# The second mixture of a two-layer decoder on one core: each tile's results scattered by POOL to token and choice rows, and loaded back in token order

## The chip, the cores and the metric

The kernel runs on one core of one Trainium2 chip. The time is device microseconds of one execution, and the median of the runs counts. Engines are named as in the profile: PE is TensorE's matmul, PEld its weight load, DVE VectorE, ACT ScalarE, POOL GpSimd, SP SyncE; SPq is SP's DMA queue.

## The reference, cut to what matters

The decoder has two layers over 1024 tokens (4 x 256) of 256 channels. All the work around this change is in its last sublayer, a mixture of 16 experts of which each token takes two, and a shared expert:

```python
logits = flat @ router_w.T
scores = jax.nn.softmax(logits, axis=-1)
_, topk_idx = jax.lax.top_k(logits + router_bias, TOPK)          # TOPK = 2
topk_scores = jnp.take_along_axis(scores, topk_idx, axis=-1)
topk_scores = topk_scores / topk_scores.sum(-1, keepdims=True)
combine = jnp.einsum('nk,nke->ne', topk_scores, jax.nn.one_hot(topk_idx, N_EXPERTS))
for e in range(N_EXPERTS):
    h = jax.nn.silu(flat @ Wu[e]) * (flat @ Wg[e])
    out = out + combine[:, e:e + 1] * (h @ Wd[e])
out = out + jax.nn.silu(flat @ Su[0]) * (flat @ Sg[0]) @ Sd[0]
x = x + out
```

## The kernel before

The program is written out by hand, one instruction stream to an engine, with semaphores between them. `PsumBanks` hands out PSUM's eight banks in the order in which PE claims them; `filled` counts PE's finished banks, in that one order, and `emptied` counts the banks read by ACT and by DVE.

The 2048 (token, choice) pairs of the second mixture are sorted by expert into 31 tiles of 128 slots (`TILES1`); each expert's slots begin at a tile, so slots are left over. DVE works out every pair's slot (`e_slot`, `e_idx`, L1922 to L1938). Two one-hot matrices, `e_A` and `e_B` (L1942 to L1947), let one PE product (`tile_tokens`, L1085) give for every slot its token, which DVE turns into `e_ids` (L1954 to L1956); the expert of each tile goes to `e_eid` (L1948 to L1951). A slot without a pair has token 0.

Then these streams run over the tiles:

- POOL (L2175 to L2185) issues one indirect DMA for each tile, which fetches its 128 token rows of 1 KB from HBM (`xs1`) into one of eight buffers `e_x`. From the ninth on it waits until PE has turned the rows that were in the buffer.
- PE (L1139 to L1147) turns tile j+1's rows, multiplies tile j by its expert's two up weights, turns the hidden rows of tile j-1, and multiplies those of tile j-2 by the down weights (`ex`, `eu`, `eh`, `ey`).
- DVE (L1975 to L1979) copies the turned rows out (`rows_out`) and multiplies gate by up (`gated_tile`). ACT (L1459 to L1465) takes the gate's Silu (`gate`), copies the turned hidden rows (`hidden_out`) and the results (`result_out`), these into one of four buffers `e_y`, for which it waits until the result four tiles back has been sent.
- SP (L2304 to L2306) stores each result, in order of slots, to `ys1` in HBM.

When all 31 results are stored, POOL issues 16 indirect DMAs, two for each of the eight token tiles, that fetch every token's two rows from `ys1` by `e_idx` into `e_yg`. DVE adds each pair with its weights to X (L1991, L1993) and SP stores that token tile.

The shared expert's down product is `shared_down(t)`: t = 0 to 3 ahead of the tile loop, t = 4 to 7 after it; DVE adds each to X (`residual`).

Of the kernel before, what the change touches and what calls it, by code (L numbers as in the profile page):

```python
# [13 lines left out]
P = 128  # L14
F32 = mybir.dt.float32
# [71 lines left out]
def decoder(nc, x, ctx_512, L0_attn_Wk, L0_attn_Wv, L0_attn_Wr, L0_attn_Wo, L0_attn_time_decay, L0_attn_time_first,  # L87
# [5 lines left out]
    with ExitStack() as ctx:  # L93
# [5 lines left out]
        def sem(name):  # L99
            return ctx.enter_context(nc.semaphore(name))  # L100
# [12 lines left out]
        def at(name, offset, shape, dt=F32):  # L113
            size = int(np.prod(shape[1:])) * 4
            assert offset + size <= room, (name, offset + size, room)
            return nc.alloc_sbuf_tensor_at(name, shape, dt, offset=arena + offset)
# [190 lines left out]
        e_hT = at("e_hT", 131072, [P, 2, P])  # L307
        e_y = at("e_y", 132096, [P, 4, C])
        e_yg = at("e_yg", 136192, [P, NT, 2, C])
        xs1 = nc.dram_tensor("token_rows_6", [B * T, C], F32, kind="Internal").ap()  # L310
        ys1 = nc.dram_tensor("tile_results_6", [TILES1 * P, C], F32, kind="Internal").ap()


        filled = sem("bank_filled")
# [33 lines left out]
        res_sent = [sem(f"slot_results_sent_{i}") for i in range(3)]  # L348
        res_back = [sem(f"token_results_loaded_{t}") for t in range(NT)]
        router_loaded = sem("router_loaded")  # L350
        xs1_stored = sem("token_rows_stored")
        choice_ready = sem("two_choices_ready")
        onehot_ready = sem("slot_one_hots_ready")
        eid_ready = sem("tile_experts_ready")
# [152 lines left out]
        def _(pe):  # L507
# [611 lines left out]
            def shared_down(t):  # L1119
                out_product(("sd", t), [(e_hs[:, it, t * P:(t + 1) * P], m_wd[:, E1 + it, :]) for it in range(2)])  # L1120
# [11 lines left out]
            pe.wait_ge(*banks.emptied(("sg", 1)))  # L1132
            for t in range(4):
                shared_down(t)
            pe.wait_ge(eid_ready, 1)
            of_tile = nc.values_load_multi_w_load_instructions(
                e_eid[0:1, 0:TILES1], engines=[mybir.EngineType.PE], min_val=0, max_val=E1 - 1,
                skip_runtime_bounds_check_because="a count of ends among the first 15 experts")[1]
            for j in range(-1, TILES1 + 2):  # L1139
# [5 lines left out]
                    hidden_turned(j - 1)  # L1145
                if 0 <= j - 2:
                    tile_down(j - 2)  # L1147
            pe.wait_ge(*banks.emptied(("sg", 3)))
            for t in range(4, NT):
                shared_down(t)  # L1150
            ended(pe, 5)


# [318 lines left out]
        def _(dve):  # L1472
            steps = [0]

            def link(ins):

                steps[0] += 1
                ins.then_inc(dve_step, 1)
                dve.wait_ge(dve_step, steps[0])
# [42 lines left out]
            def residual(key, t):  # L1522
                ps = banks.take(key, "dve")
                dve.wait_ge(*banks.filled(key))
                V.tensor_tensor(X[:, t, :], X[:, t, :], ps[:, 0:C], ALU.add).then_inc(emptied["dve"], 1)  # L1525
# [191 lines left out]
            def bcast(a, n):  # L1717
                return a.unsqueeze(2).to_broadcast([P, a.shape[1], n])
# [216 lines left out]
                                 e_rank[:, :, :].rearrange("p e t -> p t e").unsqueeze(1).to_broadcast([P, 2, NT, E1]), ALU.mult))  # L1935
            link(V.tensor_reduce(e_slot[:, :, :], e_sel[:, :, :, :], AX, ALU.add))
            slot = e_slot[:, :, :].rearrange("p k t -> p (k t)")
            link(V.tensor_copy(e_idx[:, :], slot))  # L1938
            link(V.tensor_scalar(e_qu[:, :], e_idx[:, :], P - 1, None, ALU.bitwise_and))
            link(V.tensor_copy(e_q[:, :], e_qu[:, :]))  # L1940
            link(V.tensor_tensor(e_jq[:, :], slot, e_q[:, :], ALU.subtract))
            link(V.tensor_tensor(e_one[:, :, :], bcast(e_jq[:, :], 32), e_tiles.unsqueeze(1).to_broadcast([P, 2 * NT, 32]), ALU.is_equal))  # L1942
            V.tensor_scalar(e_A[:, :, 0, :], e_one[:, :, :], e_p, None, ALU.mult)
            V.tensor_tensor(e_A[:, :, 1, :], e_one[:, :, :], bcast(e_high, 32), ALU.mult)
            for k in range(2):
                V.tensor_tensor(e_B[:, NT * k:NT * (k + 1), :], bcast(e_q[:, NT * k:NT * (k + 1)], P),
                                e_iota.unsqueeze(1).to_broadcast([P, NT, P]), ALU.is_equal).then_inc(onehot_ready, 1)  # L1947
            link(V.tensor_tensor(e_past[:, :, :], e_end[:, 0:E1 - 1].unsqueeze(1).to_broadcast([P, 32, E1 - 1]),  # L1948
                                 bcast(e_j, E1 - 1), ALU.is_le))
            link(V.tensor_reduce(e_ef[:, :], e_past[:, :, :], AX, ALU.add))  # L1950
            V.tensor_copy(e_eid[:, :], e_ef[:, :]).then_inc(eid_ready, 1)  # L1951
            ps = banks.take("ids", "dve")
            dve.wait_ge(*banks.filled("ids"))
            V.tensor_reduce(e_idf[:, :], ps[:, 0:64].rearrange("p (s j) -> p j s", s=2), AX, ALU.add).then_inc(emptied["dve"], 1)  # L1954
            dve.wait_ge(*banks.emptied("ids"))
            V.tensor_copy(e_ids[:, :], e_idf[:, :]).then_inc(ids_ready, 1)  # L1956
            for n in range(1, 4):
                hidden(n)
            for t in range(4):
                residual(("sd", t), t)  # L1960
            def rows_out(j):

                if j >= 2:
                    dve.wait_ge(*banks.filled(("eu", j - 2)))
                copy_out(("ex", j), e_xT[:, j % 2, :, :], lambda ps: ps[:, 0:2 * P].rearrange("p (k s) -> p k s", k=KC))
# [9 lines left out]
            for j in range(-1, TILES1):  # L1975
                if j + 1 < TILES1:
                    rows_out(j + 1)
                if j >= 0:
                    gated_tile(j)  # L1979
            for t in range(4, NT):  # L1980
                residual(("sd", t), t)
            dve.wait_ge(e_exp, 2)
            link(V.tensor_tensor(e_sel[:, :, :, :], e_oh[:, :, :, :], f_e[:, :, :].unsqueeze(1).to_broadcast([P, 2, NT, E1]), ALU.mult))
            link(V.tensor_reduce(e_s[:, :, :], e_sel[:, :, :, :], AX, ALU.add))
# [2 lines left out]
            link(V.tensor_tensor(e_w[:, :, :], e_s[:, :, :], e_sum[:, :].unsqueeze(1).to_broadcast([P, 2, NT]), ALU.mult))  # L1987
            for t in range(NT):
                dve.wait_ge(*banks.emptied(("sd", t)))
                dve.wait_ge(both_back[t], 32)  # L1990
                V.scalar_tensor_tensor(X[:, t, :], e_yg[:, t, 0, :], e_w[:, 0, t:t + 1], X[:, t, :], ALU.mult, ALU.add).then_inc(both_added, 1)  # L1991
                dve.wait_ge(both_added, t + 1)
                V.scalar_tensor_tensor(X[:, t, :], e_yg[:, t, 1, :], e_w[:, 1, t:t + 1], X[:, t, :], ALU.mult, ALU.add).then_inc(x_final, 1)  # L1993
# [4 lines left out]
        def _(pool):  # L1998
# [173 lines left out]
            link(G.memset(y_wop[:, :, :, :], 0.0))  # L2172
            for ot in range(KC):
                G.tensor_copy(y_wop[:, ot, :, 0:16], y_wo[:, ot, :].rearrange("p (h d) -> p h d", h=H)).then_inc(wo_padded, 1)
            pool.wait_ge(xs1_stored, 32)  # L2175
            pool.wait_ge(ids_ready, 1)
            for j in range(TILES1):
                if j >= 8:
                    pool.wait_ge(*banks.filled(("ex", j - 8)))
                G.indirect_dma_start(e_x[:, j % 8, :], None, xs1, IndirectOffsetOnAxis(ap=e_ids[:, j:j + 1], axis=0)).then_inc(tile_back[j % 8], 16)  # L2180
            for i in range(4):
                pool.wait_ge(tile_sent[i], 16 * len(range(i, TILES1, 4)))
            for t in range(NT):
                for k in range(2):
                    G.indirect_dma_start(e_yg[:, t, k, :], None, ys1, IndirectOffsetOnAxis(ap=e_idx[:, k * NT + t:k * NT + t + 1], axis=0)).then_inc(both_back[t], 16)  # L2185
            ended(pool, 5)


# [1 line left out]
        def _(sp):  # L2190
# [109 lines left out]
            for g in range(2):  # L2300
                sp.wait_ge(hn_ready, NT * 5 + 4 * (g + 1))
                sp.dma_start(xs1[4 * g * P:4 * (g + 1) * P, :].rearrange("(t p) c -> p t c", p=P),
                             HN[5][:, 4 * g:4 * (g + 1), :]).then_inc(xs1_stored, 16)
            for j in range(TILES1):  # L2304
                sp.wait_ge(*banks.emptied(("ey", j)))
                sp.dma_start(ys1[j * P:(j + 1) * P, :], e_y[:, j % 4, :]).then_inc(tile_sent[j % 4], 16)  # L2306
            for t in range(NT):
                sp.wait_ge(x_final, t + 1)
                sp.dma_start(ov[t], X[:, t, :]).then_inc(stored, 16)
# [3 lines left out]
def shape_constants():  # L2313

    f = np.float32

    def angles(n, dim, base):
        inv = f(1.0) / np.power(f(base), np.arange(0, dim, 2, dtype=f) / f(dim), dtype=f)
        return np.arange(n, dtype=f)[:, None] * inv[None, :]

    c = {"ident_c": np.eye(P, dtype=f)}
    a = np.repeat(angles(T, QW, 10000.0), 2, axis=-1)
    cos, sin = np.cos(a), np.sin(a)

    half = QW // 2
    other = np.concatenate([sin[:, half:], -sin[:, :half]], axis=-1)
    pair = lambda t: np.tile(np.concatenate([t.T[i] for i in (slice(0, P), slice(0, P), slice(P, QW), slice(P, QW))])
                             .reshape(3, P, T).transpose(1, 0, 2), (1, 1, 2))
    c["cosq_c"], c["sinq_c"] = pair(cos), pair(other)
    a = np.zeros((LT * P, D), f)  # L2330
    a[:L] = np.repeat(angles(L, D, 10000.0), 2, axis=-1)
    sign = np.concatenate([-np.ones(D // 2, f), np.ones(D // 2, f)])
    rows = lambda t: t.reshape(LT, P, D).transpose(1, 0, 2)
    c["cosk_c"], c["sink_c"] = rows(np.cos(a)), rows(np.sin(a) * sign)
    rev = np.arange(E1, 0, -1, dtype=f)
    c["rev_c"] = np.broadcast_to(rev, (P, NT, E1))
    row = lambda a: np.broadcast_to(np.asarray(a, f), (P, len(a)))
    tri = np.triu(np.ones((P, P), f), 1)
    c["tri_c"] = np.concatenate([
        tri, row(np.arange(P)), row(P * np.arange(32)), row(np.arange(32)), np.arange(P, dtype=f)[:, None],  # L2340
        row(P * np.tile(np.arange(NT), 2)), row(P * np.arange(8)), row(np.tile(np.arange(NT) > 0, E1)), tri - 1], axis=1)
    a = angles(T, P, 1000000.0)
    rows = lambda t: np.concatenate([t, t], -1).reshape(2, P, P).transpose(1, 0, 2)
    sign = np.concatenate([-np.ones(P // 2, f), np.ones(P // 2, f)])
    c["cos1_c"], c["sin1_c"] = rows(np.cos(a)), rows(np.sin(a)) * sign
    tri = np.where(np.arange(P)[None, :] > np.arange(P)[:, None], f(NEG), f(0.0))
    c["mask_c"] = tri
    c["hmask_c"] = (np.arange(P)[:, None] // 16 % 2 == np.arange(2)[None, :]).astype(f)
    return {k: np.ascontiguousarray(v, dtype=f) for k, v in c.items()}
# [32 lines left out]
```

## Time and profile before

| | |
|---|---|
| median of 3 runs | 1368.84 us (1368.06 to 1370.04) |
| span of the profiled execution | 1379.6 us |
| busy: PE, DVE, ACT, POOL | 1272.7, 868.2, 634.6, 824.0 us |
| first fetch of a tile's rows on POOL | 1285.76 us |
| last result stored | 1354.07 us (1352.38 and 1.69) |
| first and last fetch of results on POOL | 1354.89 and 1373.67 us |

The record gives no other time of the profiled execution than its span. The span is 10.8 us above the median. Times in rows are microseconds from the span's start; "idle before" is given in square brackets with what ended it. A chain is followed back from the last instruction of the program.

### The profile page before, as it was taken

The page shows a single profiled execution, that of the slowest core. Times are in us where ns is not written, and L with a number is a line of the kernel's source. Part 1 is how long each engine was busy: PE and PEld are TensorE (multiplying, and loading weights), DVE is VectorE, ACT ScalarE, POOL GpSimd, SP SyncE. Part 2 cuts the span into 40 slices and gives each one's busy share as a digit, 9 for nine tenths or more (in the row PEclk, how much of TensorE's full clock was granted, in tenths as well). Part 3 has the DMA queues.
Part 4 walks back from the last instruction along what each step waited for, and adds up shares of the span by engine and source line. Part 5 has one row for each costly group of instructions (what it writes and reads, how often), then busy time and mean ns, then how long its engine had stood idle before and what let it go on. Part 6 is the DMA issues. An engine that isn't in the chain of part 4 may idle for free.

```text
span 1379.6 us, 20358 instructions
## 1 busy us (share of the span) xinstructions
PE 1272.7 (92%) x7123; PEld 826.8 (60%) x7123; DVE 868.2 (63%) x1490; ACT 634.6 (46%) x1687; POOL 824.0 (60%) x748
## 2 busy tenths in 40 slices
PE   7999997999999999999999758998999999989792
PEld 4865554666666666666668643445776874556582
DVE  4756666677777777778865636675666123664443
ACT  3731123445554455544551416887665115872151
POOL 1267005799999999999993445887444004560444
PEclk9999997999999999999999888999999997998897
DMA  9501111000000000000005620000000105200263
GB/s 261 134 9 32 37 31 27 9 8 9 9 11 10 9 9 9 10 11 9 9 5 176 195 65 2 1 1 1 1 1 1 27 1 155 63 1 32 69 142 118
DMA packets 66172, 58.91 MB, mean 43 GB/s; under 512 B 19424, under 2 KB 62968, under 8 KB 65560
## 3 DMA queue, kind: packets, MB, share of 16 engines
q1 hardware_dynamic: 62952, 49.09, 12.7%
q0 software_dynamic: 3120, 8.52, 2.6%
q8 instruction: 58, 0.95, 0.3%
q14 instruction: 42, 0.34, 0.1%
HBM read 40.69 MB, written 8.52 MB: 36 GB/s over the span
## 4 chain that ended last, share of the span: by engine, by line
PE 79%; DVE 6%; ACT 5%; POOL 4%; issue 4%; DMA 1%; DVEq 0%; SPq 0%; POOLq 0%; ACTq 0%
PE PS L515 73%; PE PS L523 5%; ACT s_sc L1402 2%; POOL a_m L2137 2%; POOL a_m L2131 2%; DVE s_mx L1859 1%; ACT a_m L1356 1%; DVE pm L1622 1%; DVE HN L1504 0%; PE PS L729 0%; DMA f_xg<-token_rows,f_ids 0%; POOL s_sc L2152 0%; PE PS L685 0%; POOL f_xg L2119 0%; PE PS L623 0%
## 5 line engine op out<-in xcount | busy, mean ns | idle before, releaser
L2080 POOL TENSOR_TENSOR PWS<-PWS 128x1024 f32<-128x1024 f32 x160 | 379.7, 2373 | 45.1 <-ACT PWS L1286 25.8
L1622 DVE TENSOR_REDUCE pm<-PS 128x2 f32<-128x1024 f32 x192 | 225.8, 1218 | 69.3 <-PE PS L515 68.7
L1286 ACT ACTIVATE PWS<-PS 128x512 f32<-128x512 f32 (+1 forms) x416 | 213.3, 599 | 78.4 <-PE PS L515 78.2
L515 PE MATMUL PS<-PWS,KVR 128*64 128x256 f32 (+1 forms) x1664 | 185.8, 380 | 0.0
L515 PE MATMUL PS<-QALL,KH 128*128 128x512 f32 (+1 forms) x416 | 182.6, 439 | 0.9 <-DVE QM L1646 0.9
L515 PE MATMUL PS<-QM,KL 68*128 68x512 f32 (+1 forms) x416 | 167.3, 402 | 0.0
L2152 POOL TENSOR_SCALAR s_sc<-s_sc,s_ri 128x128 f32<-128x128 f32 (+1 forms) x256 | 104.5, 429 | 98.9 <-DVE s_ri L1866 98.9
L515 PEld LDWEIGHTS PS<-PWS,KVR 128*64 128x64 f32 (+1 forms) x1664 | 121.4, 137 | 59.0 <-issue 0.9
L515 PEld LDWEIGHTS PS<-QALL,KH 128*128 128x128 f32 (+1 forms) x416 | 77.9, 187 | 76.9 <-ACT PWS L1286 57.4
L1402 ACT ACTIVATE s_sc<-PS,s_nb 128x128 f32<-128x128 f32 (+1 forms) x256 | 104.5, 433 | 3.9 <-DVE s_nb L1862 3.9
L1859 DVE TENSOR_REDUCE s_mx<-PS 128x2 f32<-128x512 f32 (+2 forms) x112 | 65.7, 611 | 50.1 <-PE PS L515 50.0
L515 PE MATMUL PS<-KH,QALL 64*128 64x512 f32 (+1 forms) x512 | 89.3, 408 | 7.0 <-DVE pm L1622 7.0
L515 PE MATMUL PS<-a_wT,HT 128*128 128x512 f32 x192 | 93.4, 620 | 0.7 <-issue 0.7
L1297 ACT ACTIVATE QALL<-CTX 128x256 fp32r<-128x256 f32 x32 | 13.3, 417 | 154.0 <-DVE CTX L1659 154.0
L515 PEld LDWEIGHTS PS<-QM,KL 68*128 68x128 f32 (+1 forms) x416 | 79.0, 190 | 6.2
L515 PEld LDWEIGHTS PS<-KH,QALL 64*128 64x128 f32 (+1 forms) x512 | 46.9, 189 | 43.7 <-issue 26.0
L515 PE MATMUL PS<-z_HTh,z_w 128*128 128x512 f32 x192 | 67.5, 420 | 2.4 <-DVEq L502 2.4
L2180 POOL DMA_INDIRECT e_x<-token_rows,e_ids x31 | 29.5, 951 | 67.2 <-DVE e_ids L1956 46.8
L2131 POOL TENSOR_TENSOR a_m<-a_m,a_m 128x512 f32<-128x512 f32 x40 | 51.0, 1276 | 29.5 <-DVE a_m L1836 29.5
L1271 ACT ACTIVATE QALL<-PS 64x512 fp32r<-64x512 f32 x32 | 19.0, 594 | 106.3 <-PE PS L515 105.9
L1525 DVE TENSOR_TENSOR X<-X,PS 128x256 f32<-128x256 f32 x40 | 16.8, 419 | 76.8 <-PE PS L515 76.7
L1390 ACT ACTIVATE s_pt<-PS 128x512 f32<-128x512 f32 x64 | 38.5, 602 | 53.6 <-PE PS L523 53.6
(328 smaller groups left out, 2518.3 us busy)
## 6 DMA issues: line engine op xcount, KB each, us to landing
QALL<-qlo SPq DMA_DIRECT2D x32, 128.0 KB, 2.4
QM<-QALL SPq DMA_DIRECT2D x64, 64.0 KB, 2.0
f_w<-in_L_ffn_w_dram SPq DMA_DIRECT2D x2, 2048.0 KB
tile_results<-e_y SPq DMA_DIRECT2D x31, 128.0 KB
a_nat<-in_L_attn_w_qkv_dram SPq DMA_DIRECT2D x1, 3072.0 KB, 13.0
x_wq<-in_L_xattn_Wq_dram SPq DMA_DIRECT2D x1, 2048.0 KB, 10.4
x_wo<-in_L_xattn_Wo_dram SPq DMA_DIRECT2D x2, 1024.0 KB, 6.9
a_wo<-in_L_attn_w_o_dram SPq DMA_DIRECT2D x1, 2048.0 KB, 17.5
```

The lines of the kernel that those rows point to most:

```text
L515: return nc.tensor.matmul(o, a, b, start=start, stop=stop, **kw)
L523: last = nc.tensor.transpose(ps[0:w, c:c + r], a, ident[0:r, 0:r])
L1286: nc.scalar.activation(PW[c][0:rows, j * HALF:(j + 1) * HALF], st_bank("block", LT * u + lt)[0:rows, :], ACT.Exp).then_inc(p_ready, 1)
L1390: nc.scalar.activation(s_pt[:, m % 2, 0, :], ps, ACT.Copy).then_inc(emptied["act_turned"], 1)
L1402: ins = nc.scalar.activation(s_sc[:, k % 4, h, 0:nk], ps[:, j * nk:(j + 1) * nk], ACT.Exp, bias=s_nb[:, k % 3, h:h + 1], scale=scale, accu ...
L1622: V.tensor_reduce(pm[u % 2][:, :, i // 3, i % 3], src, AX, ALU.max).then_inc(nat_read, 1)
L1859: ins = V.tensor_reduce(s_mx[:, k % 3, i * per:(i + 1) * per], banks.bank(key)[:, 0:per * nk].rearrange("p (h k) -> p h k", h=per), AX, AL ...
L2080: G.tensor_tensor(ACC[:, :], PW[0][:, :] if i == 0 else ACC[:, :], PW[i + 1][:, :], ALU.add).then_inc(acc_step, 1)
L2131: G.tensor_tensor(a_m1[:, n % 6, :], a_m1[:, n % 6, :], a_m2[:, n % 2, :], ALU.add).then_inc(m_sum, 1)
L2137: G.tensor_tensor(m1, m1, a_bt[:, i, s, :].unsqueeze(1).to_broadcast([P, 4, P]), ALU.add).then_inc(qk_ready, 1)
L2152: ins = G.tensor_scalar(s_sc[:, n % 4, h, 0:nk], s_sc[:, n % 4, h, 0:nk], s_ri[:, n % 4, h:h + 1], 1.0, ALU.mult, ALU.mult)
L2180: G.indirect_dma_start(e_x[:, j % 8, :], None, xs1, IndirectOffsetOnAxis(ap=e_ids[:, j:j + 1], axis=0)).then_inc(tile_back[j % 8], 16)
```

## The change

- Each result is no longer stored by SP in order of slots. POOL issues one indirect DMA for each tile that writes its 128 rows to row `choice * 1024 + token` of a larger `ys1`. To this end the one-hot product's value is now that row plus one (`scalar_tensor_tensor` for `e_A`, and a constant row that numbers the pairs 0 to 2047). A slot without a pair gives 0 and gets a row of its own behind the 2048 (`e_dump`, `e_miss`). The row to fetch is the lower ten bits (`e_tok`).
- POOL issues the first eight fetches, and then, tile by tile, the fetch of tile j+8 and the scatter of tile j-3.
- After all scatters SP loads the results with eight plain DMAs, 256 KB each, one for each token tile.
- The tile experts `e_eid` are worked out ahead of the one-hot matrices, not after them. All eight `shared_down` and their `residual` run ahead of the tile loop.

```diff
@@ tensor
             for t in range(4):
                 shared_down(t)
+            pe.wait_ge(*banks.emptied(("sg", 3)))
+            for t in range(4, NT):
+                shared_down(t)
             pe.wait_ge(eid_ready, 1)
...
-            pe.wait_ge(*banks.emptied(("sg", 3)))
-            for t in range(4, NT):
-                shared_down(t)
             ended(pe, 5)
@@ vector
-            link(V.tensor_copy(e_idx[:, :], slot))
+            V.tensor_copy(e_idx[:, :], slot).then_inc(idx_ready, 1)
+            dve.wait_ge(idx_ready, 1)
+            link(V.tensor_tensor(e_past[:, :, :], ..., ALU.is_le))
+            link(V.tensor_reduce(e_ef[:, :], e_past[:, :, :], AX, ALU.add))
+            V.tensor_copy(e_eid[:, :], e_ef[:, :]).then_inc(eid_ready, 1)
...
-            V.tensor_scalar(e_A[:, :, 0, :], e_one[:, :, :], e_p, None, ALU.mult)
+            V.scalar_tensor_tensor(e_A[:, :, 0, :], e_one[:, :, :], e_p, e_one[:, :, :], ALU.mult, ALU.add)
...
-            link(V.tensor_tensor(e_past[:, :, :], ..., ALU.is_le))
-            link(V.tensor_reduce(e_ef[:, :], e_past[:, :, :], AX, ALU.add))
-            V.tensor_copy(e_eid[:, :], e_ef[:, :]).then_inc(eid_ready, 1)
+            V.tensor_scalar(e_dump[:, :], e_tiles, e_p, float(2 * B * T + 1), ALU.add, ALU.add)
             ps = banks.take("ids", "dve")
...
-            V.tensor_copy(e_ids[:, :], e_idf[:, :]).then_inc(ids_ready, 1)
+            link(V.scalar_tensor_tensor(e_miss[:, :], e_idf[:, :], 0.0, e_dump[:, :], ALU.is_equal, ALU.mult))
+            link(V.scalar_tensor_tensor(e_idf[:, :], e_idf[:, :], -1.0, e_miss[:, :], ALU.add, ALU.add))
+            link(V.tensor_copy(e_ids[:, :], e_idf[:, :]))
+            V.tensor_scalar(e_tok[:, :], e_ids[:, :], B * T - 1, None, ALU.bitwise_and).then_inc(ids_ready, 1)
             for n in range(1, 4):
                 hidden(n)
-            for t in range(4):
+            for t in range(NT):
                 residual(("sd", t), t)
...
-            for t in range(4, NT):
-                residual(("sd", t), t)
...
-                dve.wait_ge(both_back[t], 32)
+                dve.wait_ge(both_back[t], 16)
@@ gpsimd
+            def rows_fetched(j):
+                if j >= 8:
+                    pool.wait_ge(*banks.filled(("ex", j - 8)))
+                G.indirect_dma_start(e_x[:, j % 8, :], None, xs1, IndirectOffsetOnAxis(ap=e_tok[:, j:j + 1], axis=0)).then_inc(tile_back[j % 8], 16)
+            def result_sent(j):
+                pool.wait_ge(*banks.emptied(("ey", j)))
+                G.indirect_dma_start(ys1, IndirectOffsetOnAxis(ap=e_ids[:, j:j + 1], axis=0),
+                                     e_y[:, j % 4, :], None).then_inc(tile_sent[j % 4], 16)
             pool.wait_ge(xs1_stored, 32)
             pool.wait_ge(ids_ready, 1)
-            for j in range(TILES1):
-                if j >= 8:
-                    pool.wait_ge(*banks.filled(("ex", j - 8)))
-                G.indirect_dma_start(e_x[:, j % 8, :], None, xs1, IndirectOffsetOnAxis(ap=e_ids[:, j:j + 1], axis=0)).then_inc(tile_back[j % 8], 16)
-            for i in range(4):
-                pool.wait_ge(tile_sent[i], 16 * len(range(i, TILES1, 4)))
-            for t in range(NT):
-                for k in range(2):
-                    G.indirect_dma_start(e_yg[:, t, k, :], None, ys1, IndirectOffsetOnAxis(ap=e_idx[:, k * NT + t:k * NT + t + 1], axis=0)).then_inc(both_back[t], 16)
+            for j in range(8):
+                rows_fetched(j)
+            for j in range(TILES1 + 3):
+                if j + 8 < TILES1:
+                    rows_fetched(j + 8)
+                if j >= 3:
+                    result_sent(j - 3)
@@ sync
-            for j in range(TILES1):
-                sp.wait_ge(*banks.emptied(("ey", j)))
-                sp.dma_start(ys1[j * P:(j + 1) * P, :], e_y[:, j % 4, :]).then_inc(tile_sent[j % 4], 16)
+            for i in range(4):
+                sp.wait_ge(tile_sent[i], 16 * len(range(i, TILES1, 4)))
+            for t in range(NT):
+                both = ys1[0:2 * B * T, :].rearrange("(k t p) c -> t p k c", k=2, p=P)
+                sp.dma_start(e_yg[:, t, :, :], both[t]).then_inc(both_back[t], 16)
```

## Rows read from the trace of the kernel before

**Rows 1.** The page's first line.

```profile
span 1379.6 us, 20358 instructions
```

**Rows 2.** The chain that ended last: start, length, what.

```profile
1352.38 1.69 DMA tile_results<-e_y
...
1358.64 2.76 DMA e_yg<-tile_results,e_idx
```

**Rows 3.** PE's timeline, turning of rows: start, length, line, operation, count, idle before.

```profile
1311.19 0.38 PE L523 MATMUL PS<-ident,e_x 128*128 128x128 f32 x2
...
1346.99 0.38 PE L523 MATMUL PS<-ident,e_x 128*128 128x128 f32 x2
```

**Rows 4.** POOL's timeline: fetches of rows (L2180) and of results (L2185).

```profile
1285.76 1.06 POOL L2180 DMA_INDIRECT e_x<-token_rows,e_ids  x1 [46.81 <-DVE e_ids L1956]
...
1299.64 0.95 POOL L2180 DMA_INDIRECT e_x<-token_rows,e_ids  x1 [0.30 <-issue]
1303.12 0.95 POOL L2180 DMA_INDIRECT e_x<-token_rows,e_ids  x1 [2.53 <-PE PS L523]
...
1354.89 0.95 POOL L2185 DMA_INDIRECT e_yg<-tile_results,e_idx  x1 [19.32 <-DMA tile_results<-e_y]
...
1373.67 0.95 POOL L2185 DMA_INDIRECT e_yg<-tile_results,e_idx  x1 [0.30 <-issue]
```

**Rows 5.** The timeline of all engines, fifth tile: PE's turning, DVE's copy.

```profile
1294.58 0.38 PE L523 MATMUL PS<-ident,e_x 128*128 128x128 f32 x2
...
1302.95 0.42 DVE L1486 COPY e_xT<-PS 128x256 f32<-128x256 f32 x1 [4.46 <-PE PS L523]
```

**Rows 6.** DVE's timeline from the one-hot matrices to the slots' tokens.

```profile
1279.94 0.35 DVE L1943 TENSOR_SCALAR e_A<-e_one,e_c 128x512 bf16<-128x512 bf16 x1
1280.20 0.68 DVE L1944 TENSOR_TENSOR e_A<-e_one,e_c 128x512 bf16<-128x512 bf16 x1
...
1283.08 0.65 DVE L1948 TENSOR_TENSOR e_past<-e_end,e_c 128x480 f32<-128x480 f32 x1
...
1284.54 0.22 DVE L1954 TENSOR_REDUCE e_idf<-PS 128x32 f32<-128x64 f32 x1
1284.80 0.18 DVE L1956 CAST e_ids<-e_idf 128x32 uint32<-128x32 f32 x1
```

**Rows 7.** PE's timeline ahead of the tile loop.

```profile
1283.58 0.63 PE L515 MATMUL PS<-e_A,e_B 128*128 128x64 bf16 x16
1285.62 3.72 PE L515 MATMUL PS<-m_wd,e_hs 128*128 128x256 f32 x16 [1.41 <-DVE e_hs L1902]
1289.28 0.44 PE L523 MATMUL PS<-ident,e_x 128*128 128x128 f32 x2
```

**Rows 8.** The tile view of `f_xg`, the first mixture's fetches: min/median/max ns.

```profile
L2119 POOL DMA_INDIRECT f_xg<-token_rows,f_ids x10: 945/1058/2129, 772.0 to 786.9; - x10
```

**Rows 9.** DMA issues of the whole run: count, KB each, median us to landing.

```profile
m_wd<-in_L_ffn_Wd_dram SPq DMA_DIRECT2D x1, 2048.0 KB, 8.7
```

**Rows 10.** DVE's timeline, the adds of the results.

```profile
1359.00 0.48 DVE L1991 SCALAR_TENSOR_TENSOR X<-e_yg,e_w,X 128x256 f32<-128x256 f32 x1 [1.78 <-DMA e_yg<-tile_results,e_idx]
1359.52 0.48 DVE L1993 SCALAR_TENSOR_TENSOR X<-e_yg,e_w,X 128x256 f32<-128x256 f32 x1
...
1376.96 0.48 DVE L1993 SCALAR_TENSOR_TENSOR X<-e_yg,e_w,X 128x256 f32<-128x256 f32 x1
```

**Rows 11.** DMA queue of POOL, 1280 to 1380 us: packets, MB, share of 16 engines.

```profile
q0 software_dynamic: 2256, 6.16, 27.7%
```

**Rows 12.** Windows: us, busy and count of PE, PEld, DVE, ACT, POOL, PE's clock, DMA.

```profile
1290.00:1300.00 10.00, 6.16 (x29) 4.35 (x29) 2.23 (x7) 1.11 (x4) 7.56 (x9) 0.96 0.38 106
1300.00:1310.00 10.00, 8.12 (x24) 6.01 (x25) 2.05 (x6) 3.00 (x11) 3.42 (x4) 0.53 0.38 106
```

**Rows 13.** PE's timeline, turning of rows, seventh and eighth tile.

```profile
1306.45 0.64 PE L523 MATMUL PS<-ident,e_x 128*128 128x128 f32 x2
...
1309.56 0.38 PE L523 MATMUL PS<-ident,e_x 128*128 128x128 f32 x2
```

More of the change, by code:

```diff
@@ L309, in decoder @@
         e_yg = at("e_yg", 136192, [P, NT, 2, C])
+        e_dump = at("e_dump", 144384, [P, 32])
+        e_tok = at("e_tok", 144640, [P, 32], U32)
+        e_miss = at("e_miss", 144512, [P, 32])
         xs1 = nc.dram_tensor("token_rows_6", [B * T, C], F32, kind="Internal").ap()
-        ys1 = nc.dram_tensor("tile_results_6", [TILES1 * P, C], F32, kind="Internal").ap()
+        ys1 = nc.dram_tensor("choice_results_6", [(2 * NT + TILES1) * P, C], F32, kind="Internal").ap()
         filled = sem("bank_filled")
@@ L350, in decoder @@
         router_loaded = sem("router_loaded")
-        xs1_stored = sem("token_rows_stored")
+        xs1_stored = sem("slot_rows_stored")
+        idx_ready = sem("choice_slots_ready")
         choice_ready = sem("two_choices_ready")
@@ L1937, in _ @@
             slot = e_slot[:, :, :].rearrange("p k t -> p (k t)")
-            link(V.tensor_copy(e_idx[:, :], slot))
+            V.tensor_copy(e_idx[:, :], slot).then_inc(idx_ready, 1)
+            dve.wait_ge(idx_ready, 1)
+            link(V.tensor_tensor(e_past[:, :, :], e_end[:, 0:E1 - 1].unsqueeze(1).to_broadcast([P, 32, E1 - 1]),
+                                 bcast(e_j, E1 - 1), ALU.is_le))
+            link(V.tensor_reduce(e_ef[:, :], e_past[:, :, :], AX, ALU.add))
+            V.tensor_copy(e_eid[:, :], e_ef[:, :]).then_inc(eid_ready, 1)
             link(V.tensor_scalar(e_qu[:, :], e_idx[:, :], P - 1, None, ALU.bitwise_and))
@@ L1947, in _ @@
                                 e_iota.unsqueeze(1).to_broadcast([P, NT, P]), ALU.is_equal).then_inc(onehot_ready, 1)
-            link(V.tensor_tensor(e_past[:, :, :], e_end[:, 0:E1 - 1].unsqueeze(1).to_broadcast([P, 32, E1 - 1]),
-                                 bcast(e_j, E1 - 1), ALU.is_le))
-            link(V.tensor_reduce(e_ef[:, :], e_past[:, :, :], AX, ALU.add))
-            V.tensor_copy(e_eid[:, :], e_ef[:, :]).then_inc(eid_ready, 1)
+            V.tensor_scalar(e_dump[:, :], e_tiles, e_p, float(2 * B * T + 1), ALU.add, ALU.add)
             ps = banks.take("ids", "dve")
@@ L2340, in shape_constants @@
         tri, row(np.arange(P)), row(P * np.arange(32)), row(np.arange(32)), np.arange(P, dtype=f)[:, None],
-        row(P * np.tile(np.arange(NT), 2)), row(P * np.arange(8)), row(np.tile(np.arange(NT) > 0, E1)), tri - 1], axis=1)
+        row(P * np.arange(2 * NT)), row(P * np.arange(8)), row(np.tile(np.arange(NT) > 0, E1)), tri - 1], axis=1)
     a = angles(T, P, 1000000.0)
```

## The prediction

> **What bounds the kernel now.** The span [rows 1] says what the sum is made against, and the chain that ended last [rows 2] shows where to look: behind the last result's store (1352.38 + 1.69 = 1354.07) it runs through POOL's fetches of results to the end. So I read the timelines of the last hundred microseconds, engine by engine. The reader is to see two regimes. In the tile loop PE sets the pace: 22 tiles from 1311.19 to 1346.99 are 1.627 us each [rows 3]. POOL needs less for its one fetch per tile and waits for PE. After the loop POOL sets the pace: from the first to the sixteenth fetch of results 18.78 us pass, 1.252 us each [rows 4], and DVE and SP follow at that pace.
>
> One stretch needs care. PE turned the fifth tile's rows at 1294.58, but the two that wait for this, DVE's copy [rows 5] and POOL's thirteenth fetch [rows 4], began at 1302.95 and 1303.12. Some 8 us went by, and no row names a cause. Without it the last tile, 26 tiles later, would have been turned at 1294.58 + 26 x 1.627 = 1336.9 and not at 1346.99 [rows 3]: 10.1 us. The span is 10.8 us above the median of the runs. I take this as a sign that timed executions lack the stretch: 1379.6 - 10.1 = 1369.5, 0.7 us above the median of 1368.84. Below, 1369.5 stands for the kernel before, and what I work out for the changed one is lowered by 0.7.
>
> **What comes ahead of the tiles.** The three tile-expert operations now run before the one-hot matrices: 1283.08 to 1284.54 is 1.46 us [rows 6]. `e_A`'s first half becomes a three-operand instruction; bounds are its present 0.35 and the 0.68 of its neighbour of the same size [rows 6], and I take the neighbour, +0.33. The one-hots so end 1.79 later, at 1284.9. The tile experts had hidden PE's wait for them: the product ended at 1283.58 + 0.63 = 1284.21 [rows 7], the reduction began at 1284.54. With half of the 16 products (0.32) behind the later one-hots it begins at 1285.4, 0.9 later. Three more linked steps follow, each like reduction to cast, 0.26 [rows 6]: 0.78. `e_dump` is hidden behind the product. POOL's first fetch moves from 1285.76 [rows 4] by 1.7 to 1287.4 (bounds: +0.8, if only the steps count; +2.6, if nothing is hidden).
>
> PE's eight `shared_down` start 1.7 later, too, and the four that are moved ahead double 3.72 [rows 7]: 1285.62 + 1.7 + 7.44 = 1294.7 for the first turning, against 1289.28. At the end they cost nothing before: POOL's fetches hid them. Now they hide behind POOL as well, if the next step holds.
>
> **POOL in the loop.** It loses 16 fetches and gains 31 scatters. The trace has no scatter. Its nearest rows are fetches with the same 128 rows of 1 KB and the same column of indices: 0.95 us, 1.252 from one to the next [rows 4]. The first mixture's ten took 0.945 to 2.129, median 1.058 [rows 8]; nothing excludes less than 0.945. I take 1.252. A tile then costs POOL 2.504 us, more than PE's 1.627, and POOL becomes the bound. It issues twelve fetches before its first scatter, until 1287.4 + 12 x 1.252 = 1302.4. The first result needs four steps of PE behind 1294.7, 6.5 us: 1301.2. So POOL doesn't wait there, and issues 62 DMAs without a break: the last begins at 1287.4 + 61 x 1.252 = 1363.8. What is queued behind POOL: `result_out` on ACT waits until the scatter four tiles back has landed, and ACT's gates stand behind it, so PE keeps at most three tiles ahead. After the last fetch (51st issue, 1350.0) eleven scatters come at 1.252; eight results are due in that time, 13.0 us at PE's pace against 13.8, so POOL still doesn't wait. PE, ACT and DVE are hidden behind POOL throughout; SP's 31 stores, removed, were hidden but for the last.
>
> On the transfers: POOL's 47 DMAs took 27.7% of 16 engines in 100 us, 0.59 us each [rows 11], half of what their issue takes. The Trainium skill, page "DMA: Bandwidth & Descriptors", section "Issuing engines are not separate DMA queues", says that all DMAs run on the same 16 engines, and that the sequencer's time to start one, which other issuing engines would save, is usually small beside the DMA itself. By it the move of 31 stores to POOL would cost next to nothing, and the sum would be the faster rival's below; the rows say that here the issue is the larger part.
>
> **The end.** The last scatter lands like a fetch, 2.76 after its start [rows 2]: 1366.6 (a store landed in 1.69, a lower bound). SP then loads. The first 256 KB I take at the same 2.76: 1369.3. All 2 MB may take the 8.7 of another 2 MB load [rows 9], until 1375.3. DVE's two adds for a token tile start 0.52 apart [rows 10], 1.03 a tile, 8.24 in all, until 1377.6; that is later than the last load and its pair, so DVE sets this stretch. From the last add's end, 1376.96 + 0.48, to the span's end were 2.16 us [rows 10, 1]. Sum: 1379.7, 10.2 above 1369.5. In the removed part 16 fetches of 1.252, 20.0 us, are gone; POOL's 46 extra issues in and beyond the loop give back more.
>
> **Rivals.** *Faster: issue does not bound.* If a fetch and a scatter together take POOL no more than 1.627, PE bounds the loop. The last result, 1354.07 - 10.1 - 1.69 = 1342.3 before, comes 5.4 later (1294.7 for 1289.28): 1347.7. With 0.3 to start, 2.76 to land, and 13.2 for loads, adds and store (2.76 + 8.24 + 2.16) the end is 1364.0, the time 1363.3. For: the transfer's 0.59. Against: sixteen and thirty-one issues that all took 0.95. Break-even lies at a last scatter begun at 1353.6, which is 1.085 an issue. This is what that page's rule would give.
>
> *The unexplained stretch is real.* If timed runs have it before and after, the first result comes at 1309.2, POOL waits 6.8, and the span is 1386.5 against 1379.6: +6.9, 1375.7. If only the changed kernel has it: 1385.8. If only the old one has it, 1379.7 meets 1379.6: no change, 1368.9. For: ten issues in a row came before it, and POOL now issues in a row throughout. Against: the median.
>
> *PE's clock.* With 1.627 of work in 2.504 PE is 65% busy. Ahead of 1300 it was busy 6.16 of 10 us, and the granted clock was 0.53 in the next ten [rows 12], nearly all at the lower of its two levels (1.2 of 2.4 GHz). There two tiles were 3.11 apart [rows 13], more than 2.504. Ten such microseconds in the steady part cost 10 x (1 - 2.504/3.11) = 1.9 of PE's lead of up to 7.5, so nothing. Behind 1350.0, where PE must follow at 1.627, they cost 10 x (1 - 1.627/3.11) = 4.8: 1383.8. Low for all tiles: 1294.7 + 31 x 3.11 + 9.3 for the pipeline's three steps + 2.76 + 13.2 = 1416.
>
> *A dearer scatter.* At the first mixture's median of 1.058 [rows 8], 31 x 0.11 = 3.4 more: 1382.4; at its longest, 37 more.
>
> **How the numbers follow.** The forecast is POOL's chain without a break, 1379.7 - 0.7 = 1379.0; chance 0.58, own range 1374 to 1384 (an issue 5% cheaper or dearer is 3.9 us, the head's bounds +-0.9). The stretch in the changed kernel, with or without the old: 0.10. The clock: 0.13. A dearer scatter: 0.07. The stretch in the old alone: 0.05. Issue that does not bound: 0.07. A difference under 0.2%, 2.7 us, is about what a measurement of this kernel can't tell from none. Faster has the last case, 0.07. Same has the stretch in the old alone and an issue near break-even, 0.05 + 0.03, the latter from the forecast's own share. The rest is slower, 0.85. The range 1371 to 1388 leaves out the faster case, the old stretch and the worse half of the clock's, 0.18.
>
> **What would show it.** POOL's timeline: first fetch near 1287.4, then 62 indirect DMAs 1.25 apart, last near 1364, with no waits for PE or ACT; a scatter near 0.95. ACT's wait ahead of `e_y` ended by scatters, PE with idle time in each tile of about 2.5. The first load issued near 1366.6, adds 1.03 apart by DVE. Wrong, if scatters are much shorter or longer than fetches, if POOL waits for `ey` (then PE's clock or late signals are the bound), or if the loads outlast DVE's adds.

## The result and the profile after

The changed kernel took 1374.55 us, median of 9 runs (1369.60 to 1381.81), the kernel before beside it 1368.69 us, median of 9 (1362.76 to 1370.04). The ratio on record, formed from runs on the same chip, is 1.0076, 95% interval 1.0051 to 1.0101: slower by 0.5 to 1.0%, about 10 us. The two medians themselves are only 5.9 us apart, so the direction is clear and the size is better read from the ruler below. Predicted were 1379.0 us, a range of 1371 to 1388, and slower with a chance of 0.85. Two executions of the experiments, 1539.00 us with the plain stores and 1635.32 us with the shared products moved in the kernel before, ran at a much lower mean clock of TensorE than all others (0.78 and 0.73) and count in no median and no ratio here.

GpSimd's timeline in the changed kernel (L2187 fetches a tile's rows, L2192 scatters a tile's results), which answers to [rows 4]:

```profile
1284.63 1.05 POOL L2187 DMA_INDIRECT e_x<-token_rows,e_tok  x1 [46.11 <-DVE e_tok L1965]
1285.99 0.95 POOL L2187 DMA_INDIRECT e_x<-token_rows,e_tok  x1 [0.30 <-issue]
...
1298.51 0.95 POOL L2187 DMA_INDIRECT e_x<-token_rows,e_tok  x1 [0.30 <-PE PS L527]
1299.76 1.01 POOL L2192 DMA_INDIRECT choice_results<-e_y,e_ids  x1 [0.30 <-ACT e_hT L1171]
...
1347.35 0.97 POOL L2187 DMA_INDIRECT e_x<-token_rows,e_tok  x1 [0.30 <-issue]
1348.62 0.99 POOL L2192 DMA_INDIRECT choice_results<-e_y,e_ids  x1 [0.30 <-issue]
...
1362.68 0.97 POOL L2192 DMA_INDIRECT choice_results<-e_y,e_ids  x1 [0.30 <-issue]
```

The bracket is the idle time ahead of an instruction. Behind the first fetch none of the 61 others has more than 0.31 us there, whatever is named as the releaser: GpSimd never waits for a result. From the first start to the last are 78.05 us, 1.280 an issue.

What stood behind it: the view of waits of the changed kernel from 1280 to 1380 us (total, times, longest), TensorE's turnings two tiles apart in its timeline, and two windows of 10 us (busy time of PE, PEld, DVE, ACT and POOL, TensorE's granted clock, DMA share, GB/s).

```profile
DVE e_h L1983 <- ACT e_st L1449: 42.6, 30, 2.7
ACT e_y L1171 <- DMA choice_results<-e_y,e_ids: 35.7, 25, 2.6
PE PS L527 <- DVE e_h L1983: 9.9, 15, 1.4
POOL e_x L2187 <- PE PS L527: 5.2, 17, 0.3
```

```profile
1311.60 0.38 PE L527 MATMUL PS<-ident,e_x 128*128 128x128 f32 x2
...
1314.19 0.38 PE L527 MATMUL PS<-ident,e_x 128*128 128x128 f32 x2
...
1316.79 0.38 PE L527 MATMUL PS<-ident,e_x 128*128 128x128 f32 x2
```

```profile
1320.00:1330.00 10.00, 7.64 (x36) 5.25 (x35) 2.49 (x8) 2.88 (x12) 7.56 (x9) 1.00 0.31 106
1330.00:1340.00 10.00, 7.63 (x36) 5.18 (x36) 2.48 (x8) 2.89 (x12) 7.56 (x9) 1.00 0.31 97
```

A tile took TensorE 1.627 us in [rows 3]; here it is 2.59, about the time of two issues (0.97 + 0.99 + 2 x 0.30 = 2.56), and TensorE idles. The wait reaches it the way that the prediction named: ScalarE's copy into `e_y` waits 25 times for the scatter that still reads that buffer, the gates stand behind it on ScalarE, VectorE's gated product `e_h` waits 30 times for a gate, and TensorE's turning of those hidden rows waits for `e_h`. The granted clock is 1.00 in every window from 1280 to 1360.

The end, from SyncE's and VectorE's timelines:

```profile
1365.23 3.94 SPq L2326 DMA_DIRECT2D e_yg<-choice_results  x8
```

```profile
1368.23 0.48 DVE L1999 SCALAR_TENSOR_TENSOR X<-e_yg,e_w,X 128x256 f32<-128x256 f32 x1 [4.66 <-DMA e_yg<-choice_results]
...
1375.62 0.48 DVE L2001 SCALAR_TENSOR_TENSOR X<-e_yg,e_w,X 128x256 f32<-128x256 f32 x1
```

From the last scatter's start, 1362.68, to the end of the span, 1378.6, are 15.9 us.

The first line of its page gives that span:

```profile
span 1378.6 us, 20354 instructions
```

It is 1.0 us shorter than that of [rows 1]. The old profile holds the stretch of 10.1 us that the prediction had taken out, as the first experiment shows, and its work ahead of the second mixture ended 2.8 us later; together that is 12.9 us, against the 11.9 that the change costs by the ruler below.

**A ruler.** The work ahead of the second mixture ends at a different time in each execution: the reduction that gives the slots, `e_slot`, began between 1263.68 and 1277.92 us in the ten profiles of this study. So beside the times I compare, in one profile each, three lengths: A, from the start of that reduction to the first fetch of rows; B, from there to the start of GpSimd's last indirect DMA; C, from there to the end of the span. In the changed kernel A is 9.48, B 78.05, C 15.92, in all 103.45 us, from this first line of VectorE:

```profile
1275.15 0.42 DVE L1940 TENSOR_REDUCE e_slot<-e_sel 128x16 f32<-128x256 f32 x1
```

The ruler has its own error. A is 9.48 or 9.49 in the five profiles with the same steps in it, but C, with the same steps, was 15.92, 15.95, 15.86 and 16.9 in four, and a lower clock of TensorE, seen below, is worth up to 1.7 us. I take a difference of less than 2 us between two single profiles for shown only where rows name the steps that make it.

### The profile page after: what moved, and what is told of

The parts are those of the page before. It is cut to its first block, busy times and chain, and to the rows that moved or that the text cites. A ratio compares the mean times of both kernels' runs of the same rounds, so it can differ in the third digit from the quotient of the medians.

```text
span 1378.6 us, 20354 instructions
## 1 busy us (share of the span) xinstructions
PE 1273.2 (92%) x7123; PEld 824.7 (60%) x7123; DVE 866.8 (63%) x1494; ACT 632.3 (46%) x1687; POOL 839.4 (61%) x763
## 4 chain that ended last, share of the span: by engine, by line
PE 78%; DVE 6%; POOL 5%; ACT 5%; DMA 3%; issue 3%; DVEq 0%; POOLq 0%; SPq 0%; ACTq 0%
PE PS L519 72%; PE PS L527 5%; ACT s_sc L1406 2%; POOL a_m L2145 2%; DMA choice_results<-e_y,e_ids 2%; POOL a_m L2139 2%; DVE s_mx L1863 1%; ACT a_m L1360 1%; DVE pm L1626 1%; POOL e_x L2187 1%; DVE HN L1508 0%; PE PS L733 0%; DMA f_xg<-token_rows,f_ids 0%; POOL s_sc L2160 0%; POOL choice_results L2192 0%
## 5 line engine op out<-in xcount | busy, mean ns | idle before, releaser
L2187 POOL DMA_INDIRECT e_x<-token_rows,e_tok x31 | 29.9, 965 | 55.3 <-DVE e_tok L1965 46.1
```

## The experiments

All kernels of one group ran on one chip with the kernel before beside them, in five rounds. The first group is the kernel before again, the plain stores, the half scatters and the ring of eight; the second is the other four. The changed kernel itself did not run again in them, so what is said against it goes by the ratios and by the ruler.

**The kernel before, unchanged.** No edit.

> The kernel before, unchanged, against itself: what two series of one program differ by, and whether the unexplained stretch ahead of the fifth tile (8 us) comes again in its profile. If the stretch is rare, the span is near 1369 - 2 us and the fifth tile's copy on DVE follows PE's turning by about 0.1 us; if it belongs to this kernel, its fifth tile is copied about 8 us late again. Difference from before: 0 +- 3 us either way.

Measured: ratio 1.0012 (0.9990 to 1.0033), median 1364.32 us. In its profile the fifth tile was turned on TensorE and copied by VectorE 0.49 us apart; in [rows 5] over 8 us lie between the two:

```profile
1288.58 0.38 PE L523 MATMUL PS<-ident,e_x 128*128 128x128 f32 x2
```

```profile
1289.07 0.42 DVE L1486 COPY e_xT<-PS 128x256 f32<-128x256 f32 x1 [0.23 <-PE PS L523]
```

Here are VectorE's first line of the ruler, GpSimd's first and last fetch, and the page's span:

```profile
1272.01 0.42 DVE L1936 TENSOR_REDUCE e_slot<-e_sel 128x16 f32<-128x256 f32 x1
```

```profile
1279.84 1.06 POOL L2180 DMA_INDIRECT e_x<-token_rows,e_ids  x1 [45.69 <-DVE e_ids L1956]
...
1357.67 0.95 POOL L2185 DMA_INDIRECT e_yg<-tile_results,e_idx  x1 [0.30 <-issue]
```

```profile
span 1363.6 us, 20358 instructions
```

A is 7.83, B 77.83, C 5.93: 91.59 us. From first fetch to end are 83.76; the old profile had 1379.6 - 1285.76 = 93.84 [rows 1, 4], and 83.7 without 10.1. The stretch belonged to that one execution. TensorE's granted clock is 1.00 here in every window of 10 us from 1280 to 1340; in the old profile it was 0.53 from 1300 to 1310 [rows 12]. Against this profile the changed kernel is longer by 103.45 - 91.59 = 11.9 us: A 1.65, B 0.22, C 9.99. The ratio of 1.0076 is worth 10.4 us, with 7.0 to 13.8 as its interval.

That B hardly changed is the sum of two things: 62 issues without a pause now, 31 fetches at TensorE's pace, a wait of 19.3 us for results and 16 fetches then. C grew because the results' fetches, which had been inside B with the adds running alongside, gave way to loads and adds that begin behind GpSimd's last issue.

**Plain stores.** The scatters are gone; SyncE stores each tile's results in slot order.

```diff
-                if j >= 3:
-                    result_sent(j - 3)
...
+            for j in range(TILES1):
+                sp.wait_ge(*banks.emptied(("ey", j)))
+                sp.dma_start(ys1[j * P:(j + 1) * P, :], e_y[:, j % 4, :]).then_inc(tile_sent[j % 4], 16)
```

> The changed kernel with its 31 scatters left out: SP stores the results plainly in order of slots, as before, and the plain loads at the end read rows that are not the tokens' (the output is another). Everything else stays, the head of the tile loop and the end included. Issue theory (POOL's 62 indirect DMAs in a row set the time): POOL issues only 31, PE is the bound at 1.63 us a tile, and the time is 5 us below before, 15 below the changed kernel (1359 to 1366). Head theory (the later first tile and the eight shared products ahead of it cost what the change lost): it stays 4 to 10 us above before. End theory (the plain loads cost more than the 16 fetches): it stays above before as well, with more than 16 us from the last store to the end.

Measured: ratio 0.9959 (0.9939 to 0.9979), median 1358.86 us. With 31 issues fewer GpSimd waits for TensorE again, and a tile takes 1.63 us (its timeline):

```profile
1321.34 0.95 POOL L2187 DMA_INDIRECT e_x<-token_rows,e_tok  x1 [0.68 <-PE PS L527]
1322.96 0.95 POOL L2187 DMA_INDIRECT e_x<-token_rows,e_tok  x1 [0.68 <-PE PS L527]
1324.59 0.95 POOL L2187 DMA_INDIRECT e_x<-token_rows,e_tok  x1 [0.68 <-PE PS L527]
```

From the reduction (1271.70) to the end (1357.2) are 85.5 us, 18.0 below the changed kernel and 6.1 below the kernel before. What the end alone gains is thus 6 us net of the longer head; with the scatters on GpSimd it is taken back threefold. The 85.5 us hold a slower piece of TensorE, the eight shared products, which took 7.17 us in the changed kernel:

```profile
1281.06 8.86 PE L519 MATMUL PS<-m_wd,e_hs 128*128 128x256 f32 x32 [1.79 <-DVE e_hs L1906]
```

The granted clock was 0.56 and 0.58 from 1281.7 to 1285.7, nearly all at the lower level, though TensorE had done the same before as in the changed kernel, where it stayed at 1.00. As TensorE is the bound here, the 1.7 us are in the length, and at the clock of the changed kernel it would be some 84 us (an estimate from these two rows).

**Plain fetches.** The opposite half: SyncE brings the rows, GpSimd issues the scatters alone.

```diff
-            for j in range(8):
-                rows_fetched(j)
-            for j in range(TILES1 + 3):
...
+            for j in range(TILES1):
+                result_sent(j)
...
+            for j in range(TILES1):
+                if j >= 8:
+                    sp.wait_ge(*banks.filled(("ex", j - 8)))
+                sp.dma_start(e_x[:, j % 8, :], xs1[(j % NT) * P:(j % NT + 1) * P, :]).then_inc(tile_back[j % 8], 16)
```

> The changed kernel with the other half of GpSimd's list taken away: SyncE brings each tile's 128 rows by a plain transfer of a block of the token rows, at the same place and behind the same waits, and GpSimd issues the 31 scatters alone. The tiles get other rows, so the output is another; the work on each is the same. Theory A (the 62 issues on one engine bound the loop): one scatter a tile takes 1.27 us against TensorE's 1.627 us, so TensorE sets the pace, the last scatter starts right behind the last result, and the end follows some 16 us later as it did: as with the plain stores, about 5 us below the kernel before (ratio 0.996) and 14 to 15 us below the changed one. Theory B (the scatters are what costs, by their landing and the ring of four result tiles that they hold): they are all still there, and the time stays within 2 us of the changed kernel (ratio 1.007).

Measured: ratio 0.9983 (0.9963 to 1.0003), median 1359.57 us. The tile view of `e_y` and the page's span:

```profile
L2186 POOL DMA_INDIRECT choice_results<-e_y,e_ids x31: 958/958/1110, 1297.7 to 1345.1; - x31
...
  ACT e_y L1171: 76.9, 28
```

```profile
span 1360.8 us, 20355 instructions
```

All 31 scatters are there, and GpSimd waits for ScalarE's results 28 times. TensorE sets the pace again, 17 tiles in 27.67 us or 1.63 each:

```profile
1310.97 0.38 PE L527 MATMUL PS<-ident,e_x 128*128 128x128 f32 x2
...
1338.64 0.38 PE L527 MATMUL PS<-ident,e_x 128*128 128x128 f32 x2
```

The reduction began at 1275.07, so 85.7 us to the end: 17.7 below the changed kernel. By the ratios it is 0.9983 against 1.0076, some 13 us; the expected 0.996 lies just outside the interval. The ruler puts this kernel 5.9 us below the kernel before, the ratio 2.3, and no run says where the rest goes. Theory B falls by either: with all scatters in place the loop runs at TensorE's pace, and against the plain stores they cost some 2 us by the ruler (85.7 against the estimate of 84). It is two issues a tile on one engine that cost the time.

**Half scatters.** Each scatter sends the first 64 of its 128 rows; the rest of the rows that are read at the end are filled ahead of the loop.

```diff
-                G.indirect_dma_start(ys1, IndirectOffsetOnAxis(ap=e_ids[:, j:j + 1], axis=0),
-                                     e_y[:, j % 4, :], None).then_inc(tile_sent[j % 4], 16)
+                G.indirect_dma_start(ys1, IndirectOffsetOnAxis(ap=e_ids[0:P // 2, j:j + 1], axis=0),
+                                     e_y[0:P // 2, j % 4, :], None).then_inc(tile_sent[j % 4], 16)
```

> The changed kernel, but each scatter takes only the first 64 of its 128 rows; the other half of the results is left out, and the rows that are so not written hold the normalised inputs, which SP stores there early. The number of issues stays at 62. If POOL's time for an indirect DMA is by the row, a scatter falls from 0.99 to about 0.5 us, a tile from 2.57 to about 2.1, and the time by 31 x 0.49 = 15 us, to some 4 us below before. If it is by the DMA, scatters stay at 0.95 to 1.0 and the time within 2 us of the changed kernel (+8 to +11 over before). If the transfer into HBM were the bound, half the bytes would lower the time with the scatters' issue unchanged.

Measured: ratio 1.0076 (1.0048 to 1.0105), median 1373.67 us. The tile view of `e_y`, minimum, median and maximum in ns; the first line is the changed kernel's, the second that of the half scatters:

```profile
L2192 POOL DMA_INDIRECT choice_results<-e_y,e_ids x31: 967/989/1013, 1299.8 to 1362.7; - x31
```

```profile
L2192 POOL DMA_INDIRECT choice_results<-e_y,e_ids x31: 896/909/923, 1300.5 to 1361.1; - x31
```

Half the rows and half the bytes take GpSimd 0.08 us less of 0.989. B is 1361.05 - 1285.32 = 75.7 us, 2.3 below the changed kernel, about the 31 x 0.08 = 2.5 that the shorter scatters make. So the price is nearly all per DMA, as far as these two sizes tell.

**A ring of eight.** Eight buffers of results in place of four, so that ScalarE need not wait for a scatter's landing.

```diff
-        e_y = at("e_y", 132096, [P, 4, C])
+        e_y = at("e_y", 152576, [P, 8, C])
...
-                if j >= 4:
-                    act.wait_ge(tile_sent[j % 4], 16 * (j // 4))
+                if j >= 8:
+                    act.wait_ge(tile_sent[j % 8], 16 * (j // 8))
```

> The changed kernel with eight result buffers in place of four, so that ACT, which waited 25 times for a scatter to land, may run seven tiles ahead. Issue theory: POOL is busy without a break either way, so ACT's and PE's waits move or vanish, and the time stays that of the changed kernel, within 2 us. Ring theory (the wait of ACT for the scatter four tiles back, 2.4 us after its issue, holds the loop): PE then runs at 1.63 us a tile and the time falls by 5 us or more.

Measured: ratio 1.0104 (1.0074 to 1.0133), median 1375.27 us. ScalarE's wait is gone (the view of waits), the time is not:

```profile
ACT e_y L1171 <- DMA choice_results<-e_y,e_ids: 1.2, 1, 1.2
PE PS L527 <- DMA e_x<-token_rows,e_tok: 7.3, 9, 1.8
```

TensorE waits for fetched rows instead, which come from the same engine's list. A is 9.49, B 78.01, C 15.95, in all 103.45 us, as in the changed kernel, although the shared products took 8.86 us here too. The 35.7 us on ScalarE were the shadow of the bound.

**The shared products put back, in the changed kernel.** `shared_down` and `residual` of the last four token tiles stand behind the loop again.

```diff
-            pe.wait_ge(*banks.emptied(("sg", 3)))
-            for t in range(4, NT):
-                shared_down(t)
             pe.wait_ge(eid_ready, 1)
...
+            pe.wait_ge(*banks.emptied(("sg", 3)))
+            for t in range(4, NT):
+                shared_down(t)
```

> The changed kernel with only the last four shared products and their residual sums back behind the tiles' loop, where they stood before. Theory A (GpSimd's issues bound the loop, TensorE and VectorE have time to spare in it): nothing is given back, ratio 1.006 to 1.009 to the kernel before. Rival (the products put ahead of the loop are what costs, 16 matmuls of 0.232 us each or 3.7 us on TensorE): 3.7 us are given back, ratio 1.005.

Measured: ratio 1.0115 (1.0079 to 1.0150), median 1375.52 us; from the reduction (1263.68) to the end (1367.2) 103.5 us. Nothing is given back.

**The same move alone, in the kernel before.** All eight shared products and sums ahead of the loop.

```diff
+            pe.wait_ge(*banks.emptied(("sg", 3)))
+            for t in range(4, NT):
+                shared_down(t)
             pe.wait_ge(eid_ready, 1)
```

> The kernel before with only that move made: all eight shared products and residual sums ahead of the loop, everything else as it was. Here TensorE sets the loop's pace, and the work that the products hid under (the results' fetches at the end) is left empty: 3.7 us slower, at most 5, ratio 1.002 to 1.004. If the move is free in the kernel before too, 1.000.

Measured: ratio 1.0024 (0.9991 to 1.0058), median 1363.11 us, which alone doesn't tell it from no change. The one profile does: reduction at 1266.25, first fetch at 1274.09, end at 1360.7, so A is 7.84 as before and the rest 86.61 against 83.76: +2.85 us, below the 3.7 expected. Its steps agree: TensorE turned the last tile's rows 61.91 us behind the reduction (1328.16), in the kernel before 58.91 (1330.92). Here, where TensorE is the bound, the move costs; in the changed kernel, where GpSimd is, it is free.

**The tile-expert steps put back.** The three VectorE operations `e_past`, `e_ef` and `e_eid` stand behind the one-hots again.

```diff
-            link(V.tensor_tensor(e_past[:, :, :], e_end[:, 0:E1 - 1].unsqueeze(1).to_broadcast([P, 32, E1 - 1]),
-                                 bcast(e_j, E1 - 1), ALU.is_le))
-            link(V.tensor_reduce(e_ef[:, :], e_past[:, :, :], AX, ALU.add))
-            V.tensor_copy(e_eid[:, :], e_ef[:, :]).then_inc(eid_ready, 1)
...
+            link(V.tensor_tensor(e_past[:, :, :], e_end[:, 0:E1 - 1].unsqueeze(1).to_broadcast([P, 32, E1 - 1]),
+                                 bcast(e_j, E1 - 1), ALU.is_le))
+            link(V.tensor_reduce(e_ef[:, :], e_past[:, :, :], AX, ALU.add))
+            V.tensor_copy(e_eid[:, :], e_ef[:, :]).then_inc(eid_ready, 1)
```

> The changed kernel with the three steps of VectorE that find each tile's expert put back behind the one-hots. Theory A: the slots are known some 1.4 us earlier, GpSimd's chain starts and ends so much earlier, and TensorE, busy with the shared products until after that, waits for nothing new: 1.4 us below the changed kernel (ratio about 1.0065), too little for the times alone to tell; in the trace the stretch from the reduction that gives the slots to the first fetch falls from 9.5 to about 8.1 us, and the stretch from the first fetch to the end stays at 94.0 us. Rival (TensorE needs the experts early): the second stretch grows by what the first loses.

Measured: ratio 1.0098 (1.0067 to 1.0130), median 1376.87 us, so the times show no gain. A is 1277.70 - 1268.66 = 9.04, only 0.44 below the changed kernel, and this expectation was wrong where the prediction had been right: put back, the three steps stand in VectorE's list ahead of the reduction `e_idf` and hold it up themselves. VectorE's timeline there:

```profile
1275.59 0.18 DVE L1956 CAST e_eid<-e_ef 128x32 uint32<-128x32 f32 x1
1275.68 0.23 DVE L1957 TENSOR_SCALAR e_dump<-e_c 128x32 f32<-128x32 f32 x1
1275.83 0.22 DVE L1960 TENSOR_REDUCE e_idf<-PS 128x32 f32<-128x64 f32 x1
```

`e_idf` follows with no wait for TensorE; in the changed kernel it waited 0.35 us:

```profile
1282.76 0.22 DVE L1960 TENSOR_REDUCE e_idf<-PS 128x32 f32<-128x64 f32 x1 [0.35 <-PE PS L519]
```

B is 78.02, unchanged. C is 16.9, 1.0 more. VectorE's adds waited 0.17 and 0.95 us for the third and fourth load of results, where in the changed kernel they waited 0.37 for the third, so 0.75 of it; I have no cause for that, and it was seen in this one profile.

## Why the prediction was right

**The bound.** Right: 62 issues without a pause set the loop. Each of the two halves taken off GpSimd's list brings back about 18 us by the ruler, and 16 and 13 by the ratios, although one of them leaves all fetches and the other all scatters in place. A longer ring, TensorE's work or fewer bytes bring at most 3. The price of an issue was too low: 61 x 1.252 = 76.4 us were predicted, 78.05 measured. The scatter, which no row of before showed, took 0.989 us in place of the fetch's 0.95, and the fetches between scatters 0.97. This 1.7 us is the difference between the predicted 10.2 us and the 11.9 of the ruler.

**The head.** Right, by its steps: the reduction `e_idf` was to start 0.9 later and three linked steps to add 0.78. `e_A`'s first half took 0.75 us, above the upper bound of 0.68 by a little. Behind `e_slot` the reduction began 1282.76 - 1275.15 = 7.61 us, before 1284.54 - 1277.92 = 6.62, so 0.99 later; from there to the first fetch the three steps added 0.66, and A grew by 1.65 in all. (The prediction's own terms, 1284.9 and 0.32, give 1285.2 for the reduction; the 1285.4 that it wrote has 0.2 us without a term.) TensorE's eight shared products took 7.17 us in its timeline (predicted 7.44):

```profile
1284.51 7.17 PE L519 MATMUL PS<-m_wd,e_hs 128*128 128x256 f32 x32 [1.79 <-DVE e_hs L1906]
1291.52 0.60 PE L527 MATMUL PS<-ident,e_x 128*128 128x128 f32 x4
```

That they cost nothing behind GpSimd's list, and something where that cover is gone, is what the two kernels with the moved products show (0 and 2.85 us).

**The end.** The sum was right to 0.1 us (15.9), by luck, as its terms were less so and cancel: the scatter landed in 2.4 us, not 2.76, with the load issued 2.55 behind its start; the first add came 3.0 behind the first load's issue, not 2.76; the adds took 7.87, not 8.24, at 0.92 for a token tile in place of 1.03 and with one wait of 0.37 for the third load; and from the last add's end to the span's end were 2.50, not 2.16.

**The base.** Taking 10.1 us out of the old span was the largest choice of the sum, and the repeated profile bears it out: 83.76 us from first fetch to end against 83.7. Without that choice 1379.7 would have met 1379.6, and the forecast would have been no change, 10 us lower. Part of the stretch can be read: behind some 2.5 us without work TensorE's granted clock was 0.50, the lower level, from 1300 to about 1308, and tiles were turned at 1301.45, 1306.45 and 1309.56, so two tiles at that clock took 4.9 us of the 10.1, a wait of 1.44 us for VectorE's late copy included. Why TensorE and VectorE stood still before it stays open; it came in one of the two profiles of that kernel, and in no other profile does a length of the ruler show it.

**The rivals.** *Issue does not bound* fell: the break-even of 1.085 us an issue is below every issue seen. The Trainium skill, page "DMA: Bandwidth & Descriptors", section "Issuing engines are not separate DMA queues", says that the time to start a DMA is usually small beside the DMA itself. This case's trace does not agree: an issue with its pause took 1.28 us where a scatter landed 2.4 us behind its start, and the 16 DMA engines were busy for 0.31 of the windows shown while GpSimd, which issues, had no free time. With the tiles' rows brought as often, but from SyncE's list, about 18 us came back by the ruler. *TensorE's clock* did not come about in the changed kernel: TensorE was busy 7.4 to 8.0 of 10 us in the steady part, and the granted clock stayed 1.00, the higher level. Ahead of the loop, in the shared products, it did fall for some 4 us in four of the ten profiles (plain stores, ring of eight, shared products put back, tile-expert steps put back). In the three of these where GpSimd sets the pace it moved nothing, as the prediction said of its lead: B is 78.01, 78.17 and 78.02, 78.05 without it. *A dearer scatter* holds in part, by 0.04 us each and not 0.11. *The unexplained stretch* was not in the changed kernel's profile.

**The time.** 1374.55 lies 4.5 us below the forecast, though the ruler's difference is 1.7 above it. The part of the program ahead of the second mixture moves by more than that from one execution to the next (14 us between the extremes of ten profiles), so the medians can't judge a term of 2 us, and I read nothing from it.

**Slips.** The last fetch is the 50th issue and twelve scatters follow it, not the 51st and eleven; "46 extra issues" are 31 more in the loop and 15 more in all (62 against 47). The sum uses neither.

## What to carry to other kernels

Count the indirect DMAs on the engine that issues them, with the pause between two: when that sum in a loop's step passes the step's longest compute engine, as 2.56 us passed 1.63 here, the issuing engine sets the pace, however idle the DMA engines are, and what a transfer saves at the end has to be set against that in every step. A wait seen on a downstream engine can be a shadow of that list: the ring of eight took away 34.5 us of ScalarE's waiting and no time. And where the rest of a program varies by more than the effect, measure from a landmark just ahead of the change to the end.

## What the runs showed that was not expected

In this loop an indirect DMA's price on GpSimd hardly depended on its rows: a scatter took 0.989 us for 128 rows, 0.909 for 64, at the same place; a line through these two would put 0.83 us on the DMA and 1.25 ns on a row. It differed a little with its neighbours: a scatter took 0.989 us between fetches, 0.967 behind scatters alone at the end of the same loop, and 0.958 where no fetch was issued; a fetch took 0.94 to 0.95 among fetches and 0.97 between scatters. No run tells why, and none tells why TensorE's clock fell in the shared products in some profiles and not in others.
